# Cross-attention in four-head groups with no tile skipped

## The reference

```python
x = x + _L0_xattn_ref(_layernorm(x), ctx_1024, mask, Wq, bq, Wk, bk, Wv, bv, Wo, bo)
x = x + _L0_attn_ref(_layernorm(x))
x = x + _L0_ffn_ref(_layernorm(x), gate_W, ...)
```

## Time and profile before

| what | value |
|---|---|
| median of 3 runs (lowest, highest) | 182.79 us (182.25, 182.9) |
| profiled execution, time | 183.04 us |
| profiled execution, span of the trace | 181.2 us |
| TensorE matmul busy | 129.4 us, 71% |
| VectorE busy | 117.5 us, 65% |
| ScalarE busy | 55.1 us, 30% |
| GpSimd busy | 50.2 us, 28% |
| mean granted TensorE clock | 0.831 |

### The profile page before, as it was taken

The page is one execution under the profiler, slowest core; times in us unless marked ns, Lnnn a source line. Parts: engine busy times, 40 slices in busy tenths (PEclk is TensorE's granted clock), DMA queues, the critical chain, the costliest instruction groups (busy, mean ns, idle before and its releaser), DMA issues.

```text
span 181.2 us, 2776 instructions
## 1 busy us (share of the span) xinstructions
PE 129.4 (71%) x893; PEld 101.6 (56%) x893; DVE 117.5 (65%) x379; ACT 55.1 (30%) x147; POOL 50.2 (28%) x64
## 2 busy tenths in 40 slices
PE   0768666247789845983006279999999999879990
PEld 0434323113248635752005278998997897779980
DVE  2269969988599000067898768977845469998114
ACT  2132202002022720541432017047002569862110
POOL 1281400000000000003086000077376007977400
PEclk9999969855555995699555558999999999999996
DMA  5999996000000000009920000000000000001042
GB/s 166 199 453 405 416 406 222 0 4 0 0 5 0 4 5 4 0 4 347 463 118 0 0 0 0 4 1 2 6 1 4 0 0 25 15 22 33 22 127 63
DMA packets 7177, 16.05 MB, mean 89 GB/s; under 512 B 1440, under 2 KB 5760, under 8 KB 6640
## 3 DMA queue, kind: packets, MB, share of 16 engines
q1 hardware_dynamic: 5936, 14.80, 21.5%
q10 hardware_dynamic: 576, 0.42, 1.5%
q0 software_dynamic: 640, 0.51, 1.1%
HBM read 14.44 MB, written 1.38 MB: 87 GB/s over the span
## 4 chain that ended last, share of the span: by engine, by line
PE 52%; DVE 29%; issue 9%; ACT 3%; DMA 2%; POOL 1%; DVEq 1%; ACTq 0%; SPq 0%
PE A L937 10%; PE C L822 8%; DVE arena L1138 7%; PE D L993 7%; PE C L925 5%; PE A L749 5%; PE D L773 3%; DVE arena L1475 3%; PE A L972 3%; DVE arena L1144 3%; DMA arena<-ctxT 2%; ACT arena L615 2%; DVE x L1302 2%; PE D L982 2%; PE A L952 1%
## 5 line engine op out<-in xcount | busy, mean ns | idle before, releaser
L615 ACT ACTIVATE arena<-C 128x512 f32<-128x512 f32 x22 | 12.5, 596 | 37.4 <-PE C L822 37.4
L749 PE MATMUL A<-arena 32*128 32x512 f32 x64 | 13.7, 940 | 10.5 <-DVE mxb L1138 7.2
L539 POOL DMA_INDIRECT y_table<-arena,slot x12 | 16.9, 1408 | 14.7 <-DVE arena L1495 11.6
L488 POOL TENSOR_SCALAR vare<-mv 128x2 f32<-128x2 f32 (+3 forms) x7 | 1.9, 268 | 67.2 <-DVE mv L1089 67.2
L937 PE MATMUL A<-arena,kw 128*128 128x161 f32 x128 | 18.8, 301 | 0.3 <-DVE arena L1424 0.3
L993 PE MATMUL D<-arena 128*128 128x161 f32 x128 | 18.6, 301 | 0.4 <-DVE arena L1475 0.4
L1138 DVE CUSTOM_DVE_ANT_0 arena<-A,arena,mxh 128x512 f32<-128x512 f32 x24 | 16.6, 747 | 3.5 <-PE A L749 3.5
L937 PEld LDWEIGHTS A<-arena,kw 128*128 128x128 f32 x128 | 17.7, 189 | 1.3 <-DVE arena L1424 0.7
L993 PEld LDWEIGHTS D<-arena 128*128 128x128 f32 x128 | 17.7, 189 | 0.9 <-issue 0.7
L822 PE MATMUL C<-cst,arena 128*128 128x128 f32 x88 | 16.3, 346 | 2.2 <-issue 1.7
L822 PEld LDWEIGHTS C<-cst,arena 128*128 128x128 f32 x88 | 13.3, 181 | 7.3 <-issue 5.0
(11 more groups left out here) (195 smaller groups left out, 239.9 us busy)
## 6 DMA issues: line engine op xcount, KB each, us to landing
kw<-KW SPq DMA_DIRECT2D x1, 4096.0 KB, 16.2
arena<-KW SPq DMA_DIRECT2D x1, 4096.0 KB, 12.9
mw<-MW SPq DMA_DIRECT2D x2, 1024.0 KB, 19.3
arena<-ctxT SPq DMA_DIRECT2D x4, 256.0 KB, 8.2
arena<-mask SPq DMA_DIRECT2D x1, 768.0 KB, 8.6
y_table<-zeros SPq DMA_DIRECT2D x1, 512.0 KB, 20.5
arena<-y_table SPq DMA_DIRECT2D x2, 256.0 KB, 3.0
xs<-x SPq DMA_DIRECT2D x1, 256.0 KB, 2.9
```

The source lines that it names most:

```text
L539: pool.indirect_dma_start(out=y_table, out_offset=bass.IndirectOffsetOnAxis(ap=slot[0:m, j, n, 0:1], axis=0), in_=yn[0:m, n, j], in_offset ...
L615: act.activation(PT[:, k % 2, g * 512:(g + 1) * 512], C[g][:, :], ACT.Exp).then_inc(probsT_kept, 1)
L749: last = mm(BANK[j], QM[32 * j:32 * j + 32, u, b], kT[32 * j:32 * j + 32, b], start=True, stop=True)
```

## The change

The tail is computed without branches. Work is cut in 8 groups n = 2b + u of four heads, and each group in 4 tiles, m = 4n + t. `transposes(m)` makes 4 transposes into C[m % 2], `exponentials` one exp into one of now four `PT` buffers, and `mix(m)` follows `transposes(m + 2)`. Scores are issued two groups ahead of the tiles. The maximum is taken for each group by itself over the tail alone. Of a group's four heads VectorE shifts the last two, and ScalarE the first two, between its exponentials. All keys and values are made before the first tile.

The head of the masks is no longer looked at before the tail is done. One flag (is there any unmasked key in the head?) is made while group 3 is worked on and read behind the tail. If it is set, the head is streamed once with a running maximum and joined to the tail's result; otherwise that code is passed over. The tail tiles that had no key are now computed.

GpSimd's memsets of the values' pads move to its start. SP loads contexts 1 to 3 ahead of the masks' head and of the second part of the constants.

```diff
-        PT = part(2 * H * P, "p (u n) -> p u n", u=2)
+        PT = part(4 * 4 * P, "p (u n) -> p u n", u=4)
...
+        h_out = S[:, 2, 0:2].rearrange("p h k -> p (h k)").rearrange("p (b n) -> p b n", b=B)
...
-            sp.dma_start(cst[:, C_FIRST:], consts[:, C_FIRST:]).then_inc(cst_in, 16)
-            sp.dma_start(mask_u8[:, :, 0:HEAD * P], mask[:, :, 0:HEAD * P]).then_inc(mask_head_in, 16)
             for b in range(1, B):
                 sp.dma_start(ctx_t[:, b], ctxT[b, :, HEAD * P:]).then_inc(ctx_in[b], 16)
+            sp.dma_start(mask_u8[:, :, 0:HEAD * P], mask[:, :, 0:HEAD * P]).then_inc(mask_head_in, 16)
+            sp.dma_start(cst[:, C_FIRST:], consts[:, C_FIRST:]).then_inc(cst_in, 16)
...
+            for v in (V.rearrange("p b t h w -> p (b t h) w"), h_V):
+                nc.gpsimd.memset(v[:, :, HD + 1:], 0.0).then_inc(pads_made, 1)
+                nc.gpsimd.memset(v[:, :, HD:HD + 1], 1.0).then_inc(pads_made, 1)
...
-                if b == 1:
-                    for v in (V.rearrange("p b t h w -> p (b t h) w"), h_V):
-                        nc.gpsimd.memset(v[:, :, HD + 1:], 0.0).then_inc(pads_made, 1)
-                        nc.gpsimd.memset(v[:, :, HD:HD + 1], 1.0).then_inc(pads_made, 1)
...
-            nc.gpsimd.memset(oT[:, 2:], 0.0).then_inc(oT_cleared, 1)
...
+            keep_keys_values(3)
+
+            def shift(n, heads=(0, 1)):
+                b, u = divmod(n, 2)
+                act.wait_ge(heads_max, n + 1)
+                for h in (4 * u + j for j in heads):
+                    act.activation(S[:, b % SBUFS, h], S[:, b % SBUFS, h], ACT.Identity, bias=nmxb[:, b, h:h + 1], scale=1.0
+                                   ).then_inc(shifted_act, 1)
+
+            def exponentials(n):
+                for t in range(TAIL):
+                    m = n * TAIL + t
+                    if m >= 4:
+                        act.wait_ge(mixed, m - 3)
+                    act.wait_ge(probsT_made, m + 1)
+                    act.activation(PT[:, m % 4], C[m % 2][:, :], ACT.Exp).then_inc(probsT_kept, 1)
+                    if t < 2 and n + 1 < GROUPED:
+                        shift(n + 1, (t,))
+
+            shift(0)
+            for n in range(GROUPED):
+                exponentials(n)
+
+            word = load_word(act)
+            with act.If(word > 0):
+                with act.Fori(0, STREAMED) as i:
...
-            def exponentials(k):
-                def body():
-                    if k >= 2:
-                        act.wait_ge(mixed, k - 1)
...
-                        act.wait_ge(probsT_made, 2 * k + g + 1)
-                        act.activation(PT[:, k % 2, g * 512:(g + 1) * 512], C[g][:, :], ACT.Exp).then_inc(probsT_kept, 1)
-                when(act, tail[k], body, [(probsT_kept, 2)])
...
+            def mix_heads(sums, g, v, probsT):
+                for j in range(4):
+                    last = mm(sums[VW * j:VW * (j + 1), g * P:(g + 1) * P], v[:, 4 * g + j],
+                              probsT[:, j * P:(j + 1) * P], start=False, stop=True, skip_group_check=True)
+                return last
+
+            def transposes(m):
+                n, t = divmod(m, TAIL)
+                b, g = divmod(n, 2)
+                if t == 0:
+                    pe.wait_ge(shifted_dve, 2 * n + 2)
+                    pe.wait_ge(shifted_act, 2 * n + 2)
+                if m >= 2:
+                    pe.wait_ge(probsT_kept, m - 1)
+                for j in range(4):
+                    last = nc.tensor.transpose(C[m % 2][:, j * P:(j + 1) * P], S[:, b % SBUFS, 4 * g + j, t * P:(t + 1) * P], ident)
+                last.then_inc(probsT_made, 1)
+
+            def mix(m):
+                n, t = divmod(m, TAIL)
+                b, g = divmod(n, 2)
+                if g == 0 and t == 0:
+                    if b >= 2:
+                        pe.wait_ge(oT_kept, b - 1)
+                    open_sums(b)
+                pe.wait_ge(probsT_kept, m + 1)
+                mix_heads(OV[b % 2], g, V[:, b, t], PT[:, m % 4]).then_inc(mixed, 1)
+
+            def tiles(n):
+                for m in range(n * TAIL, (n + 1) * TAIL):
+                    transposes(m)
+                    if m >= 2:
+                        mix(m - 2)
+
+            def to_queries(b):
+
+                pe.wait_ge(oT_kept, b + 1)
+                for g in range(2):
+                    last = nc.tensor.transpose(BANK[b][:, g * P:(g + 1) * P], oT[:, b, g * P:(g + 1) * P], ident)
+                last.then_inc(o_tok, 1)
 
             scores(0, 0)
             pe.wait_ge(qm_last, 2)
             pe.wait_ge(qm_first, 2)
             keys_values(1)
             scores(0, 1)
+            keys_values(2)
+            keys_values(3)
+            pe.wait_ge(pads_made, 4)
             pe.wait_ge(ones_made, 4)
+            pe.wait_ge(kv_kept, 2 * B)
+            scores(1, 0)
+            tiles(0)
+            scores(1, 1)
+            tiles(1)
             pe.wait_ge(flags_made, 1)
+            mm(D[1][0:1, 0:B], ones[:, 0:1], flags[:, 0], start=True, stop=True).then_inc(anyq_made, 1)
+            scores(2, 0)
...
+            tiles(2)
+            scores(2, 1)
+            tiles(3)
+            scores(3, 0)
+            tiles(4)
+            scores(3, 1)
+            tiles(5)
+            tiles(6)
+            pe.wait_ge(scores_kept, GROUPED)
+            to_queries(0)
+            to_queries(1)
+            tiles(7)
+            to_queries(2)
+            mix(GROUPED * TAIL - 2)
+            mix(GROUPED * TAIL - 1)
+
+            word = load_word(pe)
+            with pe.If(word > 0):
+                pe.wait_ge(probsT_kept, GROUPED * TAIL)
+                with pe.Fori(0, STREAMED) as i:
...
+                n = 2 * b + u
+                dve.wait_ge(scores_made, n + 1)
                 if u == 0:
                     dve.wait_ge(bias_made, b + 1)
-                    if b >= SBUFS:
-                        dve.wait_ge(probsT_made, 2 * TAIL * (b - SBUFS + 1))
-                        dve.wait_ge(shifted, 2 * (b - SBUFS + 1))
+                if b >= SBUFS:
+                    dve.wait_ge(probsT_made, TAIL * (n - 2 * SBUFS + 1))
+                    dve.wait_ge(shifted_dve, 2 * (n - 2 * SBUFS + 1))
+                    dve.wait_ge(shifted_act, 2 * (n - 2 * SBUFS + 1))
                 for j in range(4):
                     h = 4 * u + j
-                    start, top = (mxh[:, b, h:h + 1], mxb[:, b, h:h + 1]) if b else (-NEG, mx0[:, h:h + 1])
-                    last = v.tensor_tensor_reduce(S[:, b % SBUFS, h], BANK[j], mbias[:, b], 1.0, start, ALU.add, ALU.max, top)
+                    last = v.tensor_tensor_reduce(S[:, b % SBUFS, h], BANK[j], mbias[:, b], 1.0, -NEG, ALU.add, ALU.max, mx0[:, b, h:h + 1])
                 last.then_inc(scores_kept, 1)
 
             def shift(b, u):
-                dve.wait_ge(scores_kept, 2 * b + u + 1)
-                for h in range(4 * u, 4 * u + 4):
-                    last = v.tensor_scalar(S[:, b % SBUFS, h], S[:, b % SBUFS, h], mxb[:, b, h:h + 1], None, ALU.subtract)
-                last.then_inc(shifted, 1)
+                n = 2 * b + u
+                dve.wait_ge(scores_kept, n + 1)
+                four = slice(4 * u, 4 * u + 4)
+                v.tensor_scalar(nmxb[:, b, four], mx0[:, b, four], -1.0, None, ALU.mult).then_inc(heads_max, 1)
+                dve.wait_ge(heads_max, n + 1)
+                for h in (4 * u + 2, 4 * u + 3):
+                    v.tensor_scalar(S[:, b % SBUFS, h], S[:, b % SBUFS, h], nmxb[:, b, h:h + 1], None, ALU.add).then_inc(shifted_dve, 1)
...
             keep_scores(0, 0)
+            shift(0, 0)
+            keep_scores(0, 1)
+            shift(0, 1)
+            keep_scores(1, 0)
+            shift(1, 0)
+            dve.wait_ge(mask_in, 16)
             dve.wait_ge(mask_head_in, 16)
-            own(v.tensor_reduce(flags[:, :, 0:HEAD], mask_i32[:, :, 0:HEAD], AX, ALU.max))
+            words = mask_f.bitcast(I32).rearrange("p (b w) -> p b w", b=B)
+            own(v.tensor_reduce(flags[:, 0], words[:, :, 0:HEAD * P // 4], AX, ALU.max))
+            own(v.tensor_reduce(flags[:, 1], words[:, :, HEAD * P // 4:], AX, ALU.max))
             own_done()
             v.tensor_scalar(flags[:], flags[:], 0.0, None, ALU.is_gt).then_inc(flags_made, 1)
-            keep_scores(0, 1)
-            dve.wait_ge(cst_in, 16)
-
+            dve.wait_ge(flags_made, 1)
+            own(v.tensor_tensor(notwipe[:], flags[:, 0], flags[:, 1], ALU.max))
+            keep_scores(1, 1)
+            shift(1, 1)
             dve.wait_ge(anyq_made, 1)
-            anyq = D[1][0:1, 0:B * TILES].rearrange("p (b t) -> p b t", b=B)
-            own(v.tensor_copy(anyf[:, 0:B * TAIL].rearrange("p (b t) -> p b t", b=B), anyq[:, :, HEAD:]))
-            own(v.tensor_reduce(anyf[:, B * TAIL:], anyq[:, :, 0:HEAD], mybir.AxisListType.XY, ALU.max))
-            own_done()
-            own(v.scalar_tensor_tensor(anyf[:], anyf[:], 1.0, powers, ALU.min, ALU.mult))
```

(24 more changed lines are left out.)

## The result

The changed kernel takes 168.18 us (median of 4 runs, 167.63 to 168.34) beside 182.52 (181.23 to 182.9) on the same chip: a ratio of 0.922, 95% interval 0.917 to 0.927. Faster as forecast and inside the range, but 4 us above the 164.0, and also above the 161.5 to 166.5 that the prediction gave to its likeliest case. The profiled execution is 167.63 with a span of 165.8.

The account below looks back on a forecast made before the run. The prediction took TensorE's waits and half-rate clock in the 63 us attention as the bound. Its steps moved `den` from 77.9 to 59.0, so 183.0 less 18.9 gave 164.1, stated as 164.0 us; range 161 to 170.

Parts of the forecast that it names:

- Start, 1.0: At the kernel's start, moving GpSimd's memset gains 1.0 us (between 0 and 1.3); score group (0,0) is read from 14.0.
- First transposes, 23.5: In the attention on TensorE, the first transpose comes at 23.5 us, after early scores and all keys and values.
- Holds of 0.5 before scores (2,0), word at 33.8: VectorE's work holds scores (2,0) 0.5 us, to 33.3; group 2's tiles wait for the skip-head flag word until 33.8.
- Half tile, 0.85: TensorE's transposes and mixes for four heads take 0.85 us a tile, ends 0.80 and 0.96; 4.5 a group with scores.
- ScalarE and VectorE keep up: Per attention group, VectorE needs 3.5 us and ScalarE 3.2 to 3.5 (4.5 with hand-overs), against TensorE's 4.5.
- Three zero fills, 0.6: At the attention's end on TensorE, three zero fills of the sums take 0.6 us, before `den` at 59.0.
- Branch hidden: Behind the tail, the untaken head-streaming branch costs zero; TensorE has from 59.6 to 61.4 us to cover it.
- Behind `den`, 103.2 unchanged: Everything after VectorE's `den` takes as long as before, 103 us.
- Clock at 1.00 from 23 to 60: TensorE's granted clock stays at full 2.4 GHz through the attention, with a longest gap of about 1 us.
- Rivals 1 and 2: TensorE's clock: 1, lower throughout the attention, 191 us, chance 0.04; 2, falls once or twice, 168 with two, chance 0.15.
- The trade: In the attention, removed skips, word's wait and slow clock outweigh five added tile steps, about 8.0 us of work.
- the fourth rival: ScalarE or VectorE instead of TensorE paces the attention groups, 0.96 us a half tile: 167.5 us; chance 0.17.

Follow-up runs that it names:

- e0: The changed kernel itself, unaltered, run a second time in another set: 169.22 us, ratio 0.939 to the kernel before.
- e9: Changed kernel with transposes and mixes in pairs of tiles, mask reductions spread out and the word made behind group 7: 167.33 us, ratio 0.934.
- e10: e9 with ScalarE's two shifts of the next group behind its exponentials of tiles 1 and 2 instead of 0 and 1: 165.81 us, ratio 0.910.
- e12: e10 plus throwaway matmuls on zeros in TensorE's idle times behind the attention: 164.43 us, ratio 0.898.
- e1: Changed kernel with transposes of two tiles, then mixes of two tiles, instead of one tile at a time: 168.58 us, ratio 0.944.
- e3: Changed kernel with all four shifts of a group on VectorE and none on ScalarE: 173.08 us.
- e5: Changed kernel with the five empty tile steps left out by a fixed list, no run-time test: 167.34 us, ratio 0.930.
- e7: Kernel before with all 16 tile steps computed and no tests on tail steps, head tests kept: 178.22 us, ratio 0.990.
- e8: Kernel before with all 16 steps, no tests, no word and the streaming of the masks' head left out: 171.23 us, ratio 0.945.

## Why the prediction was right, and what it sized wrong

The profiled execution is 3.5 us over the sum (167.63 against 164.1): 2.4 at `den`, the rest behind it. Step by step:

- *Start, 1.0.* `bq` took 0.43 instead of 1.78 and the first score pass began at 14.63, 0.28 earlier. x came 0.76 later in this execution, so against its arrival 1.04 was gained (the pass began 10.17 behind the first statistics, 11.21 before). That is right for this execution, but no fixed gain: in e0 the pass began 10.73 behind the statistics, and in e9, e10 and e12, where the first scores took TensorE 2.09 us instead of 1.14, it began 11.24 to 11.94 behind them (the rows of e10 and e12 show a clock of 1.00 there all the same). x also came at 3.98 to 4.47 in every execution with the new order of loads, and at 3.68 to 4.01 in the three with the old one; whether the order is the cause is not shown. The move of the memset was not undone alone.
- *First transposes, 23.5.* 24.04: the first score pass, expected at 14.0, was already 0.63 late by the late x. VectorE's later passes start from the same point (24.09), so this lateness was carried on to group 2.
- *Holds of 0.5 before scores (2,0), word at 33.8.* 0.58, and the word was ready at 34.2: right within 0.5, and the difference is the late start. Group 2's tiles began at 34.25 instead of 33.8.
- *Half tile, 0.85.* **The step that failed.** I took 0.80 from a step of eight heads and added a share of waits for ScalarE. There were no waits; the 0.944 is TensorE itself. Four transposes take 0.588 and eight mix matmuls 0.356, while before eight and sixteen took 1.03 and 0.57. Each change between the two kinds costs 0.144, and the change does it 32 times more: 4.6 us. Beyond the 0.85 that is 0.094 for each of the 24 half tiles from group 2 on, 2.3 us. With the 0.45 by which group 2 was late, and 0.3 less for zero fills, scores and turning back together, it makes the 2.4 that `den` is late. e1 and e10 show it: with the pairs back the step is 1.60, and with ScalarE's order mended a group falls from 4.84 to 4.27. The half tile's upper end, 0.96, held it, but that end was made from waits for ScalarE, which did not come: that the range covered the outcome is in part luck.
- *ScalarE and VectorE keep up.* Right: shifts take 0.715 at a pace of 0.62 inside the assumed 0.54 to 0.69, and ScalarE idles 1.4 a group. It has no room for a different order, though: e1's 0.24 to 0.31. And with all shifts on VectorE it did not keep up around the mask reductions (e3).
- *Three zero fills, 0.6.* 0.105 each, so 0.3.
- *Branch hidden.* Right: `den` to L858 is 2.39, as before (77.97 to 80.36).
- *Behind `den`, 103.2 unchanged.* 104.4. To the logits it is 21.04 in both; the rest came at the very end, where VectorE stands 3.63 instead of 3.24 before it uses the expert outputs that are read back, and the last transfer of the output takes 0.7 longer. Nothing in the change reaches there, and no run tells it from scatter; it is left open.
- *Clock at 1.00 from 23 to 60.* Right: 1.00 up to 66, with no idle time over 0.84 us from 22 to 61. The Trainium skill's rule (TensorE: Matmul & The Clock Gate, Part 4: PE-mode transpose), by which the full clock doesn't engage for transposes, isn't what the stretch 35 to 58 shows: four times 0.59 of a group's 4.84 us are transposes, and the clock is 1.00 throughout. No run here has a long stretch of transposes alone, so for that the trace says nothing. Rivals 1 and 2 did not occur in the changed kernel's profiled execution. e5, e3 and e9 show how near the second was: the clock was 0.50 behind waits for VectorE of 2.01 us (e5) and of 1.47 and 0.49 (e3), and at 12 to 14 us in e9, whose code is the changed kernel's up to there.
- *The trade.* I wrote that the skips, the word's wait and the slow clock outweigh the five added steps. e7 and e8 bear this out; how the gain is shared between the tail's tests and the word with the head's branches depends on the measure.

The outcome lies nearest to the fourth rival's figure, 167.5, but not by its mechanism: no engine but TensorE set the pace.

## What to carry to other kernels

A run-time test that skips work on TensorE has to pay for its own gap and for the lower clock that follows; here computing five empty steps was faster than skipping them by tests, and only 1 to 2 us slower than leaving them out by a fixed list. Before tiles are made smaller, price the change between kinds of matmul from a row in which both are short: a step cut in half need not cost half. When a wait is taken out, look at what stands still next, and at the clock behind it: 0.7 to 1.2 us were lost there in several runs. And compare executions between two marks inside the changed part, not by the time of one mark, since the start alone scattered by 2 us.

## What the runs showed of the hardware that I had not expected

- Four transposes and eight mix matmuls take 0.944 us, twice as many of each in one go 1.60: 0.144 for each change of kind, at full clock and without a wait.
- Matmuls on zeros keep the granted clock up: 1.00 over 66 to 75 us, where the engine without them idled at 0.50. They ran at 0.11 us each (80 in 8.90), and at 0.157 on average (32 in 5.01) while the clock came back.
